# Pairs of queries with a bank of their own, read-outs on ScalarE, and inverse roots by a power on GpSimd, in a two-layer attention and expert kernel

## The reference

```python
xn = layernorm(x)                                  # layer 0
q, k, v = mlp(xn)                                  # three two-layer MLPs with gelu
out = (tril(q @ k.T / scale)) @ v                  # no softmax
x = x + layernorm(out) * ln_w + ln_b + fp4_ffn(xn) # blockwise fp4 quantised, I = 352
xn = layernorm(x)                                  # layer 1
q = (xn @ Wq + bq).reshape(8, 512, 16, 64)         # 16 heads
k = xn @ Wk + bk; v = xn @ Wv + bv                 # one key and value head for all
w = softmax(q @ k.T / 8)
attn = (w @ v) @ Wo + bo
p = softmax(xn @ Wg + bg)                          # 8 experts, the best 2 of each token
x = x + attn + sum over the chosen e of p_e * (gelu(xn @ W1[e] + b1[e]) @ W2[e] + b2[e])
```

## Time and profile before

| | us |
|---|---|
| median of three runs | 1476.2 (1471.7 to 1479.8) |
| the profiled execution | 1480.5 |
| its span, first to last instruction | 1478.6 |
| TensorE busy | 1346.8 |
| VectorE busy | 1117.6 |
| ScalarE busy | 694.4 |
| GpSimd busy | 230.4 |

### The profile page before, as it was taken

How to read it: one execution, slowest core, us unless ns; L and a number is a source line. 1 busy time by engine, 2 the same in 40 slices (tenths; PEclk the granted TensorE clock), 3 DMA queues, 4 the chain that set the end, 5 groups by cost and what they waited for, 6 DMA issues and landing times.

```text
span 1478.6 us, 18582 instructions
## 1 busy us (share of the span) xinstructions
PE 1346.8 (91%) x5393; PEld 900.9 (61%) x5393; DVE 1117.6 (76%) x2736; ACT 694.4 (47%) x1185; POOL 230.4 (16%) x283
## 2 busy tenths in 40 slices
PE   4579999999999999999999999999999699989995
PEld 2346565666666656665666666666666466767653
DVE  8786888688868886888688867886787476756582
ACT  2126454534454445444544454445444457657542
POOL 4112213100120012001200120001001042443400
PEclk9569999999999999999999999999999899999998
DMA  3402433200020003000200020000000455454152
GB/s 104 96 13 92 144 118 110 78 16 23 20 83 16 23 20 82 18 23 19 80 16 26 19 80 16 27 16 27 16 19 22 152 178 169 158 186 137 60 139 62
DMA packets 68881, 100.05 MB, mean 68 GB/s; under 512 B 25584, under 2 KB 45616, under 8 KB 64816
## 3 DMA queue, kind: packets, MB, share of 16 engines
q1 hardware_dynamic: 56400, 70.73, 15.7%
q0 software_dynamic: 10192, 27.44, 6.1%
q10 hardware_dynamic: 2192, 0.71, 0.2%
HBM read 60.14 MB, written 38.44 MB: 67 GB/s over the span
## 4 chain that ended last, share of the span: by engine, by line
PE 58%; DVE 21%; issue 12%; POOL 5%; DMA 2%; ACT 1%; SPq 1%; POOLq 0%; DVEq 0%; ACTq 0%
PE bank L1313 21%; PE bank L1293 6%; PE bank L1247 6%; PE bank L1294 6%; POOL y_rows L616 5%; DVE mneg L891 5%; PE bank L1329 4%; PE bank L1157 2%; PE bank L1159 2%; PE bank L1158 2%; DVE q_lm L885 2%; PE bank L1208 1%; PE bank L1190 1%; DVE on L1086 1%; PE bank L1198 1%
## 5 line engine op out<-in xcount | busy, mean ns | idle before, releaser
L720 ACT ACTIVATE wide<-bank 128x512 f32<-128x512 f32 x512 | 304.4, 598 | 544.9 <-PE bank L1294 503.4
L1313 PE MATMUL bank<-wide,v_w 128*128 128x512 f32 x1024 | 526.1, 596 | 0.0
L891 DVE TENSOR_REDUCE mneg<-bank 128x1 f32<-128x512 f32 x512 | 348.2, 688 | 121.7 <-PE bank L1247 97.6
L1293 PE MATMUL bank<-q_hh,k_hl 128*128 128x512 f32 x512 | 366.5, 716 | 2.1 <-ACT wide L720 1.1
L1247 PE MATMUL bank<-k_hl,q_hh 128*128 128x512 f32 x512 | 206.9, 406 | 17.1 <-DVE mneg L891 13.5
L1313 PEld LDWEIGHTS bank<-wide,v_w 128*128 128x128 f32 x1024 | 189.6, 191 | 47.2 <-issue 1.4
L597 POOL DMA_INDIRECT x_rows<-xr,slot_u x64 | 67.8, 1059 | 891.7 <-DVE slot_u L972 740.2
L1294 PE MATMUL bank<-q_lm,k_h 65*128 65x512 f32 x512 | 202.2, 395 | 0.0
L1293 PEld LDWEIGHTS bank<-q_hh,k_hl 128*128 128x128 f32 x512 | 97.4, 190 | 99.6 <-issue 93.2
L1294 PEld LDWEIGHTS bank<-q_lm,k_h 65*128 65x128 f32 x512 | 97.8, 191 | 92.8 <-issue 90.3
L885 DVE SCALAR_TENSOR_TENSOR q_lm<-bank,bq,q_hh 64x512 fp32r<-64x512 f32 x128 | 94.7, 740 | 61.9 <-ACT q_hh L669 58.1
(11 more groups left out here) (230 smaller groups left out, 1858.4 us busy)
## 6 DMA issues: line engine op xcount, KB each, us to landing
w_t<-w_rows SPq DMA_DIRECT2D x23, 1024.0 KB
x_rows<-part_h POOLq DMA_DIRECT2D x65, 258.0 KB, 4.9
inv<-inverse_scratch SPq DMA_DIRECT2D x128, 128.0 KB
w_rows<-w_t SPq DMA_DIRECT2D x8, 1024.0 KB, 4.7
x_m<-x_rows SPq DMA_DIRECT2D x23, 258.0 KB
yab<-in_L_ffn_W SPq DMA_DIRECT2D x16, 256.0 KB, 5.0
yab<-y_rows SPq DMA_DIRECT2D x8, 512.0 KB, 4.3
xin<-in_L_attn_x SPq DMA_DIRECT2D x8, 256.0 KB, 3.2
```

What stands on the lines that cost most here:

```text
L720: act.activation(wide[:, st.g % WIDE, :], ps, ACT.Exp, scale=SCALE1).then_inc(wide_full, 1)
L891: dve.tensor_reduce(mneg[:, (gh // 2) % 2, col:col + 1], ps[:], X, ALU.max, negate=True)\
L1293: pe.matmul(ps, k_hl[:, n, t], q_hh[:, gh % HEADS, :], start=True, stop=False)
L1313: last = pe.matmul(ps_out[b][:], v_w[:, st.r % 2, c, :], wide[:, st.g % WIDE, :], start=(c == 0), stop=(c == TT - 1))
```

## The change

- Queries are projected in pairs, two heads side by side in 128 columns (`query`), 64 triples for 128. They have the last small bank for themselves (`Ring`), and the other uses share three. ScalarE writes each head's rounded query by two activations of 64 partitions, one step apart for the two heads, and VectorE's remainders follow one step later (`split_heads`). `HEADS` buffers grow from 4 to 6.
- ScalarE takes over: the copy of the maxima, the biases of `qt` and `kt`, the scaling of the off-diagonal `s0`, the rounding of `x` (`x_h`), and `k_h1`.
- Values and gate logits become one use `vg` with 72 columns.
- `norm` hands the variances to GpSimd, which raises them to -0.5 (`root`, placed by hand in its queue), and VectorE does one Newton step.
- The tiles are inserted after steps 15, 19 and 23 (8, 8, 7). SP loads the first rows at step 9. All eight results are loaded at step 34, into the space of the expert weights.
- In the last row, VectorE takes the reciprocals of heads 12 to 15 itself from the broadcast sums, 64 x 512 each, and the projection `wo` is in three parts.

```diff
-            self.place[name] = (n % banks, self.total[n % banks])
+            i = banks - 1 if name[0] == kind else n % (banks - 1)
+            n += name[0] != kind
...
-    HEADS = 4
+    HEADS = 6
+    QUERY_AT = 1
-    INSERT = {7: 5, 15: 6, 19: 6, 23: 6}
+    INSERT = {15: 8, 19: 8, 23: 7}
-    LAST_AFTER = ATT + 24
+    LAST_AFTER = ATT + 6
+    DIRECT = 12
+    INVERSE_AT = {DIRECT: 58, DIRECT + 1: 62, DIRECT + 2: 65, DIRECT + 3: 67}
+    LAST_NORM_AT = {8: 60, 9: 61, 10: 63, 11: 64, 12: 64, 13: 65, 14: 66, 15: 67}
+    LAST_WO_AT = [None, ATT + 1, ATT + 4]
-    BEGIN_AT = {46: "xt", 48: "k", 49: "v", 50: "gl", 58: "rk"}
+    BEGIN_AT = {46: "xt", 48: "k", 50: "vg", 58: "rk"}
-    COMBINE_AT = [38 + 3 * n for n in range(NB)]
+    LANDED_AT = 34
+    COMBINE_AT = [39 + 3 * n for n in range(NB)]
...
-        if c == TT - 1 and 0 <= gh + LEAD + 1 < H * NB:
-            events.append(("q", gh + LEAD + 1))
+        if c == QUERY_AT and h % 2 == 0 and 0 <= gh + LEAD + 1 < H * NB:
+            events.append(("q", (gh + LEAD + 1) // 2))
...
-                    if st.kind == "o" and st.k == 3:
+                    if st.kind == "o" and st.k == 9:
                         for t in range(XT):
                             load_tile_rows(t)
...
-                            if st.k == COMBINE_AT[n] - (3 if n < 2 else 2):
+                            if st.k == LANDED_AT:
                                 load_landed(n)
...
+            def root():
+                roots[0] += 1
+                pool.wait_ge(var_set, roots[0])
+                pool.tensor_tensor(rs[:, 1, :], rs[:, 0, :], power[:], ALU.pow).then_inc(root_set, 1)
...
             for j in range(2 * E):
+                if SPLIT_STEPS[j] in (33, 48):
+                    root()
...
             for n in range(1, NB):
+                if n > 1:
+                    root()
+                    root()
                 if n + 1 < NB:
                     zero(n + 1)
+                    root()
                 scatter(n)
...
+                if s == 6:
+                    for j, name in enumerate(("qt", "kt")):
+                        drain((name, n), lambda ps: act.activation(qk0[:, j, :], ps[:], ACT.Identity,
+                                                                   bias=b0[:, 3 + j:4 + j]))
+                if s == 8:
+                    for j in range(TT - 1):
+                        ps, _ = filled(act, ("s0", n, j))
+                        act.activation(s0t[:, j, P * (j + 1):], ps[:, P * (j + 1):], ACT.Identity, scale=SCALE0)\
+                           .then_inc(s0_spread, 1)
...
-                act.activation(q_hh[:, gh % HEADS, :], ps[:], ACT.Identity, bias=bq[:, gh % H:gh % H + 1])\
-                   .then_inc(qh_done, 1)
+                rows = slice(DK * (gh % 2), DK * (gh % 2) + DK)
+                for half in range(2):
+                    last = act.activation(q_hh[DK * half:DK * half + DK, gh % HEADS, :], ps[rows, :], ACT.Identity,
+                                          bias=bq[rows, gh % H:gh % H + 1])
+                last.then_inc(qh_done, 1)
...
-                link(dve.tensor_scalar(root.bitcast(U32), var.bitcast(U32), 1, None, ALU.logical_shift_right))
-                link(dve.tensor_scalar(root.bitcast(U32), root.bitcast(U32), -1.0, float(0x5F3759DF), ALU.mult,
-                                       ALU.add))
-                for n in range(3):
-                    link(dve.scalar_tensor_tensor(half, root, -0.5, root, ALU.mult, ALU.mult))
-                    link(dve.tensor_tensor(half, half, var, ALU.mult))
-                    link(dve.scalar_tensor_tensor(root, half, 1.5, root, ALU.add, ALU.mult))
+                yield tag
+                roots[0] += 1
+                dve.wait_ge(root_set, roots[0])
+                link(dve.scalar_tensor_tensor(half, root, -0.5, root, ALU.mult, ALU.mult))
+                link(dve.tensor_tensor(half, half, var, ALU.mult))
+                link(dve.scalar_tensor_tensor(root, half, 1.5, root, ALU.add, ALU.mult))
...
+                if r == NB - 1:
+                    for o, at_ in INVERSE_AT.items():
+                        if k == at_:
+                            gh = H * r + o
+                            emptied(dve, group_of[gh])
+                            dve.reciprocal(inv_d[0:DK, o - DIRECT, :], raw[DK:, gh % RAW, :]).then_inc(inverted_d, 1)
```

More of the change, by code:

```diff
@@ L186, in head_events, with split_heads, wo_at, norm_at @@
         return events
+    def split_heads(st, after):
+        if st.kind not in ("pre", "o"):
+            return None
+        at_ = TT * (H * st.r) + st.k - QUERY_AT - after
+        pair, b = divmod(at_, 2 * TT)
+        gh = 2 * pair + LEAD + 1 + b
+        return gh if b < 2 and 0 <= gh < H * NB else None
+    def wo_at(r, part):
+        if part == 0 or r < NB - 1:
+            return WO_AT[part] if part < 2 else None
+        return LAST_WO_AT[part]
+    def norm_at(r):
+        at_ = dict(enumerate(NORM_AT))
+        if r == NB - 1:
+            at_ = {**at_, **LAST_NORM_AT}
+        return at_
     def project_events(st):
-        return [("wo", r, half) for r, k in row_steps(st) for half in range(2) if k == WO_AT[half]]
+        return [("wo", r, part) for r, k in row_steps(st) for part in range(3) if k == wo_at(r, part)]
     def l0_events(st):
@@ L279, in two_layers @@
         rs = sb("rs", [P, 3, TT])
+        power = sb("power", [P, TT])
         qs = sb("qs", [P, 3, 32])
@@ L1062, in row_end @@
             def row_end(r, k):
-                for half in range(2):
-                    if k == WO_AT[half] + 1:
+                for half in range(3):
+                    if wo_at(r, half) is not None and k == wo_at(r, half) + 1:
                         ps, free = full(("wo", r, half))
-                        if half or r == NB - 1:
+                        if half == 2:
+                            read_out(dve, ("wo", r, 1))
+                        elif half or r == NB - 1:
                             kept()
@@ L1321, in second, with project @@
                 last.then_inc(second_done, 1)
[L1323 to L1324 removed]
+            def project(r, part):
+                tiles = (slice(0, 4), slice(4, 8 if r < NB - 1 else 6), slice(6, 8))[part]
+                pe.wait_ge(normed, H * r + 2 * tiles.stop)
                 def fill(ps):
                     for i in range(TT):
[L1328 to L1330 removed]
+                        for g in range(tiles.start, tiles.stop):
+                            last = pe.matmul(ps[:, P * i:P * i + P], on[:, g % (H // 4), P * i:P * i + P], wo[:, g, :],
+                                             start=(g == tiles.start), stop=(g == tiles.stop - 1))
                     return last
[L1332 removed]
+                into(("wo", r, part), fill)
             def tile_rows(t):
```

215 lines of the change are left out of this document (112 added, 103 removed).

## The result

The changed kernel takes 1542.7 us (median of four runs, 1542.4 to 1547.2), the kernel before 1474.2 (four runs): a ratio of 1.047, with a 95% interval of 1.043 to 1.050. It is slower by 68 us where 40 us less were forecast.

A forecast was written before the change was run, and what follows sets the result against it. TensorE was taken to bound the rows, VectorE's chain the prologue. Terms -51 - 9 - 4.2 - 1.3 + 20 + 10 - 2 - 3 = -40.5 took 1480.5 to 1440, 1436 as a median; range 1404 to 1458.

The forecast's parts named there:

- zero a row, and -3 to +3 as bounds: Rows 0 to 6: TensorE's new stalls of 3.6 us match some 3.6 gone, so its idle time stays.
- Rival 2: Layer 0 stretches: ScalarE and three banks become the bound, +3 us a row, 21 in all, so 1457; chance 0.17.
- Rival 3: GpSimd's power is a long software loop; VectorE comes late, TensorE stands at three full banks; at 8 us, about 1520; chance 0.07.
- Queries in pairs, -5.6, and values with gate logits, -1.7 a row: Rows 0 to 6: 64 query triples fewer and one shared values pass save TensorE 51 us in all.
- nothing stalls in the plain pattern: Plain steps: ScalarE, 0.69 us per half activation, is late by 1.4 us, but `exp` of two steps back leaves TensorE 1.85.
- Roots: 24 norms: each drops 1.6 us of VectorE instructions and waits 0.5 us for GpSimd (0.2 to 1.5); row 0, some 2 once.
- Prologue, -9 with -4 to -12: Prologue: VectorE's chain loses three exposed roots and some 3 us of other work, TensorE 1.4 + 2.5 us; -9 us.
- Last row, start: Last row: the 12.7 us wait for tile 0's rows goes, a new 11 us wait for `mrow` comes at step 8; -1.3.
- Longer runs, +20: Last row: from a run's fifth tile on, scatters set 10.3 us a tile; 11 waits with 37 us for seven with 16.7.
- All results at step 34, +10: Last row: eight loads issued at once delay `mrow`, which TensorE needs at step 40; +10 us (0 to +13).
- Tail: After the last scores: four VectorE reciprocals of 3.5 us replace inverses through DRAM; 24 us against 27.5, -3 (0 to -14).
- rivals 1 and 2: Rival 1: the last row doesn't pay for the load burst and longer runs, +30 goes, so 1406; chance 0.22.

The follow-up runs named there:

- b_three: Kernel before with only the ring changed: the small uses share three banks and the fourth stays unused; 1532.5 us (ratio 1.038).
- c_best: `c_order` plus eight tile-destination buffers, zeroing issued earlier, row 0's two roots ahead of earlier splits, first two tiles' rows loaded before the weights; 1410.0 us (0.952).
- b_pairs4: Kernel before with paired queries sharing the ring of four banks, the first head read in the query's own step; 1485.0 us (1.007).
- b_half: Kernel before with ScalarE's one 128 x 512 activation per rounded query replaced by two of 64 x 512; 1524.0 us (1.032).
- b_power: Kernel before with only the changed norm: inverse roots by a power on GpSimd and one Newton step on VectorE; 1496.0 us (1.013).
- c_order: `a_pairs4` with the first four tiles' weights loaded one by one at steps 6, 7, 8, 10 and the result loads three steps apart; 1457.5 us (0.989).
- b_to8: Kernel before with eight buffers for a tile's destinations instead of four; 1450.2 us (0.984).
- b_long: Kernel before with the 23 expert tiles in runs of 8, 8 and 7 behind steps 15, 19 and 23; 1484.8 us (1.006).
- a_pairs4: Changed kernel with all small uses, pairs included, in one ring of four banks, the first head read in the query's own step; 1465.5 us (0.993).

## Why the prediction was wrong, by its own steps

*The step that failed.* "TensorE's idle time in them (4.6 us in row 4) stays as it is", with "zero a row, and -3 to +3 as bounds". The prediction named the three banks, and asked only where ScalarE is late for them. The bank is freed by VectorE's reduction, and VectorE works parts of a norm, and products, between two reductions. It was judged "not the bound" at 80% busy. That share is an average; what counts is how long it can be away before TensorE stands, and that was one bank more than it has now. The rows show 9 us more idle time each, and `b_three` shows 4 of them, and 8 us of row, for the bank alone. Rival 2 had the place and took a fifth of the price (+3 a row, against +15.6 over the forecast's 141.4) and the wrong engine. Rival 3, the only slower one, had the wrong cause, since the power takes 1.03 us, but its picture of TensorE standing before three full banks is what the trace shows.

*A term that was missing.* The clock. Every stall was priced at its own length. Behind some of them TensorE ran at the 1.2 GHz level, which cost some 5 us in row 4. In rows 1 to 5 TensorE is busy for 143.3 us each, for 136.8 by the forecast, at a mean granted clock of 0.97: 4.7 of the 6.5 us are the clock's. `c_best` has no such stretch in its row 4.

*Queries in pairs, -5.6, and values with gate logits, -1.7 a row.* Right in TensorE's work: row 4 of `c_best` has 137.3 us of it for 144.1, 6.8 less for the forecast 7.3. The shared pass takes 1.66 us (789.48 to 791.14), as forecast. Some 0.3 of the missing 0.5 is that a step right behind a pass is shorter, 1.24 us for 1.56, and with one pass less there is one such step less. But less work for TensorE is not a shorter row by itself: `b_pairs4` gains nothing from the pairs alone.

*ScalarE.* 0.69 us for each half was right (`b_half`: 11.2 us more a row), and so was "nothing stalls in the plain pattern". The reason given (`exp` of two steps back) was only half of it: it also takes the slack between a query and its first use, without which `b_half` loses 6.7 us a row.

*Roots.* Taken at 0.5 us, with 0.2 to 1.5; measured:

```profile
L607 POOL TENSOR_TENSOR rs<-rs,power x24: 1006/1029/1042, 5.7 to 1158.1; 128x4 f32<-128x4 f32 x24
```

That is the least, median and longest duration in ns of the line. VectorE's waits for it:

```profile
DVE rs L869 <- POOL rs L607: 23.2, 18, 4.9
```

Inside the bounds, and in the rows the waits are 0.6 to 1.2 us. The first one takes 1.04 like the rest, with 1.23 us of VectorE's wait, so the 6 us that the Trainium skill (GPSIMD Engine Reference, 2.1 Instruction dispatch) gives the first call of a freshly loaded kernel are not seen here; no run shows whether this one was freshly loaded. The sum without them was the right one. What failed is "some 2 us once" in row 0, and the zeroing:

```profile
232.96 4.40 POOL L634 DMA_DIRECT2D x_rows<-part_h  x8
237.38 1.04 POOL L607 TENSOR_TENSOR rs<-rs,power 128x4 f32<-128x4 f32 x1
238.45 0.16 DVE L869 SCALAR_TENSOR_TENSOR rs<-rs 128x4 f32<-128x4 f32 x1 [4.87 <-POOL rs L607]
```

In row 0 VectorE waits 4.87 us here and 3.92 before it, where the root stands behind a split, and TensorE stalls for 5.4 and 6.7 us behind them. The prediction had asked what stands ahead of a root and named the split, but not the eight issues of 0.55 us. It never asked what the roots push back: the zeroing (`b_power`, a wait for `mrow` of 2.2 to 5.8 us in each of rows 1 to 5).

*Prologue, -9 with -4 to -12.* Measured -2.6, outside. VectorE is busy for 9.4 us less, as worked out, but stands 4.6 us for the roots and more for ScalarE's new shares: `s0t` 3.1, `x_h` 2.1. The term took work off an engine and left out the handovers.

*Last row, start.* Right: a wait of 9.8 us for `q_lm<-mrow` at step 8, for 11, and none for `x_m`. `c_order` shows that this queue has more to give, but that the rows come late next.

*Longer runs, +20.* The mechanism was right (10.3 a tile, and `b_to8` removes it), the size wrong: `b_long` has ten waits of 26.9 us in all, for 11 with 37, and its last row grows by 5.0 us. The tiles themselves take 13.8 us more (38.9 above 6.4 each, for 25.1, with 2.4 us taken off for the step that holds a run). But the sixteen steps up to step 15, tiles taken out, take 3.7 less (42.2 for 45.9, of which the forecast had 1.3), and the steps behind the last tile 4.6 less. Both came with the tiles' move; why the second did is not shown.

*All results at step 34, +10.* 7.1 us of wait at step 40, within the bounds. *Tail.* Reciprocals of 64 x 512 take 3.35 us, for 3.5 by the slope:

```profile
1515.18 3.35 DVE L1153 RECIPROCAL inv_d<-raw 64x512 f32<-64x512 f32 x1
```

The estimate of 4.3 from the Trainium skill (VectorE: DVE Perf Modes, Walkthrough) was too high, and the slope of two rows the better guide. The tail is 23.1 us, for 24.

*The sum.* The last row and the tail were forecast at +19.5 together and measured at +8.1; the prologue and rows 0 to 6 at -60 and measured at +58.7. With the ring of four (`a_pairs4`, idle 6.4 a row) the sign was the forecast one, at a quarter of the size. (The chances of the forecast and of rivals 1 and 2 add up to 0.89, not to 0.88 with a part of the rest.)

## What to carry to other kernels

Before giving one use a buffer of its own out of a shared ring, list what the releasing engine does between two releases at the worst place: a ring hides lateness, and one place less turned 4.6 us of idle time a row into 8.8 with no other edit. Of an instruction added to an in-order queue, price what it pushes back as well as what it waits for. And look for the wait whose distance is only a buffer count: eight small buffers for four gained 22 us in one kernel (1450.2 for 1472.0 beside it) and 39 in the other.

## What the runs showed of the hardware that I had not expected

In row 4 of the changed kernel a stall of 1.8 us behind one of 0.8, and one of 2.8 alone, were followed by 6.8 and 3.5 us at or near a granted clock of 0.50. The stalls of up to 1.6 us in row 4 of the kernel before were not, nor were those of 1.7 and 1.9 in row 4 of `b_three` (818, 865) and of 1.9 in row 4 of `c_best` (813), behind which the clock stayed at 1.00. The length of a stall alone doesn't tell: `b_three` ran at 0.51 from 882 to 889 behind stalls of 1.2 and 0.8. A power over 128 x 4 on GpSimd takes 1.03 us, five times a subtract of 128 x 8 (0.20). GpSimd is held for 0.55 us by each issue of a 258 KB transfer, 4.4 us for eight. A half activation of 64 partitions costs as much as a full one (0.69 us).
